# Two small rows of a fused attention kernel by DMA through device memory instead of by matmul

## What is computed

```python
# layer 0                                        # layer 1 (x is layer 0's output)
q, k = Wq@x + bq, Wk@x + bk       # 32 rows      theta = theta_w@x + theta_b;  phi = maxpool2(phi_w@x + phi_b)
v    = Wv@x + bv                  # 256 rows     g = maxpool2(g_w@x + g_b)     # 128 rows, 1024 columns
attn = softmax(q.T @ k, axis=1)   # over i       attention = softmax(theta.T @ phi, axis=-1)
x    = gamma * (v @ attn) + x                    x = gamma * (out_w@(g @ attention.T) + out_b) + x
```

## Time and profile before

| | us |
|---|---|
| median of 3 runs (2786.36 to 2790.55) | 2790.31 |
| the profiled execution | 2785.08 |
| its span, first to last instruction | 2783.3 |
| first layer of one image | 534 to 546 |
| second layer of one image (images 0 to 2; the last) | 143 to 144; 118 |

### The profile page before, as it was taken

The page is one execution under the profiler, slowest core; times in us unless marked ns, Lnnn a source line. Parts: engine busy times, 40 slices in busy tenths (PEclk is TensorE's granted clock), DMA queues, the critical chain, the costliest instruction groups (busy, mean ns, idle before and its releaser), DMA issues.

```text
span 2783.3 us, 39336 instructions
## 1 busy us (share of the span) xinstructions
PE 2693.6 (97%) x12260; PEld 2159.1 (78%) x12260; DVE 2004.2 (72%) x3303; ACT 1745.2 (63%) x3171; POOL 1956.3 (70%) x1544
## 2 busy tenths in 40 slices
PE   7999999999999999998999999999899999999988
PEld 5788888877688888887778888888767888888866
DVE  7677777767767777776776777777676777777665
ACT  5566666666756666666765566666676666666657
POOL 3677777767767767776786767777577677777768
PEclk9999999999999999999999999999999999999989
DMA  2000000012110000001211000000121000000011
GB/s 86 1 16 24 16 24 16 16 39 69 61 38 16 24 16 16 16 16 38 69 65 35 24 16 16 16 16 16 46 76 61 16 16 16 16 16 16 16 46 61
DMA packets 43194, 85.03 MB, mean 31 GB/s; under 512 B 2672, under 2 KB 2800, under 8 KB 42992
## 3 DMA queue, kind: packets, MB, share of 16 engines
q1 hardware_dynamic: 35360, 68.17, 7.2%
q10 hardware_dynamic: 7632, 14.36, 1.8%
HBM read 48.96 MB, written 33.55 MB: 30 GB/s over the span
## 4 chain that ended last, share of the span: by engine, by line
PE 87%; DVE 4%; issue 3%; ACT 3%; POOL 2%; DMA 0%; POOLq 0%; ACTq 0%; DVEq 0%
PE o_ps L821 18%; PE o_ps L824 18%; PE o_ps L825 18%; PE s_ps L798 10%; PE aux L861 9%; PE aux L835 2%; PE aux L874 2%; PE aux L870 2%; DVE mx L675 2%; PE aux L895 1%; POOL prob_l L446 1%; PE aux L839 1%; PE aux L878 1%; ACT queries L530 1%; PE o_ps L861 1%
## 5 line engine op out<-in xcount | busy, mean ns | idle before, releaser
L446 POOL TENSOR_TENSOR prob_l<-prob,prob_h 128x512 fp32r<-128x512 f32 x1280 | 1640.6, 1289 | 717.4 <-ACT prob_h L508 706.0
L505 ACT ACTIVATE prob<-s_ps 128x512 f32<-128x512 f32 x1280 | 767.3, 599 | 819.8 <-PE s_ps L798 817.2
L675 DVE TENSOR_REDUCE mx<-aux 128x1 f32<-128x512 f32 x1103 | 760.7, 690 | 424.0 <-PE aux L861 419.0
L821 PE MATMUL o_ps<-prob_h,vh 128*128 128x512 f32 x2304 | 926.8, 402 | 0.5 <-ACT prob_h L508 0.4
L824 PE MATMUL o_ps<-prob_l,vh 128*128 128x512 f32 x2304 | 904.6, 393 | 1.4 <-POOL prob_l L446 1.3
L825 PE MATMUL o_ps<-prob_h,vl 128*128 128x512 f32 x2304 | 903.1, 392 | 0.0
L637 DVE TENSOR_TENSOR acc<-prob,acc 128x512 f32<-128x512 f32 x1216 | 836.4, 688 | 26.8 <-ACT prob L505 11.4
L508 ACT ACTIVATE prob_h<-s_ps 128x512 fp32r<-128x512 f32 x1280 | 762.1, 595 | 0.0
L798 PE MATMUL s_ps<-queries,keys 128*128 128x512 f32 x1280 | 524.3, 411 | 17.9 <-DVE queries L694 10.8
L824 PEld LDWEIGHTS o_ps<-prob_l,vh 128*128 128x128 f32 x2304 | 436.7, 190 | 97.7 <-POOL prob_l L446 5.0
L825 PEld LDWEIGHTS o_ps<-prob_h,vl 128*128 128x128 f32 x2304 | 434.6, 189 | 99.7
(11 more groups left out here) (122 smaller groups left out, 1947.9 us busy)
## 6 DMA issues: line engine op xcount, KB each, us to landing
xa<-x SPq DMA_DIRECT2D x32, 512.0 KB, 3.7
spill<-xa SPq DMA_DIRECT2D x32, 512.0 KB, 2.7
xa<-spill SPq DMA_DIRECT2D x32, 512.0 KB, 3.7
y<-xa SPq DMA_DIRECT2D x32, 512.0 KB, 2.7
xp<-x ACTq DMA_DIRECT2D x26, 512.0 KB, 3.7
xp<-x SPq DMA_DIRECT2D x2, 512.0 KB, 9.1
prob<-w_in ACTq DMA_DIRECT2D x1, 576.0 KB, 5.3
wo<-w_out ACTq DMA_DIRECT2D x1, 128.0 KB, 6.1
```

Source lines behind the costliest of these rows:

```text
L446: nc.gpsimd.tensor_tensor(out=prob_l[:, i, :], in0=prob[:, i, :], in1=prob_h[:, i, :].bitcast(f32), op=ALU.subtract).then_inc(pl_ready, 1)
L505: nc.scalar.activation(prob[:, i, :], s_ps[s][:, :], ACT.Exp).then_inc(p_ready, 1)
L675: ins = nc.vector.tensor_reduce(out=dst, in_=bank[:, :], axis=AX.X, op=ALU.max)
L821: mm(o_ps[ct][:, :], value(vh, l, t, ct), prob_h[:, i, :], start=t == 0, stop=False)
```

## The change

M gets no bank for 59 of its 64 chunks, and D2 none for 59 of 64 either. For those, SP moves the values: it writes the maxima's two parts (`nm_pair`, 8 values per partition) to device memory as two rows of 512 (1024 pieces of 4 bytes), waits for the landing, and reads the two rows into rows 96 and 97 of `queries`. The reciprocals (512 pieces) go out likewise and come back as one row broadcast to 128 partitions (`rb`, 256 KB). The scores wait for the semaphore `nm_in`, VectorE's multiplication for `r_in`. SP now walks the common list, with its stores and loads at the places of `N`, `ZA` and `XL`.

In the first layer D2 moves from tile 0 to tile 4, with all that follows it up to `T1L`; M is at tile 25; the maxima end at tile 23, with two of them in tiles 0, 6 to 9 and 20 to 22. In the second layer D2 is at tile 4, Z at tiles 4 and 6, M for the next chunk at tile 0 (for chunk 1 at tile 5 of chunk 0, where its maxima have just been found). The scores matmuls take 98 rows instead of 128.

```diff
-                put(g, 1, on(Job("D2", *prev, 0), X1))
+                put(g + 4, 1, Job("D2", *prev, 0))
...
-                steps = [(i, X0) for i in range(27)] + [(i, X1) for i in range(20, 25)]
+                steps = sorted(([(0, 1, X0), (0, 1, X1)] + [(t, 3, X0) for t in range(1, 23)]
+                         + [(t, 1, X1) for t in (6, 7, 8, 9, 20, 21, 22, 23)]), key=lambda e: e[:2])
...
-                put(g + 28, 1, on(Job("M", 0, b, n + 1, 0), X1))
+                put(g + 25, 1, Job("M", 0, b, n + 1, 0))
...
-                put(g, 1, on(Job("D2", *prev, 0), X0))
+                put(g + 4, 1, Job("D2", *prev, 0))
...
-                    put(g + 2 + 2 * k, 3, on(Job("Z", *prev, k), X0))
-                    put(g + 3 + 2 * k, 3, Job("ZA", *prev, k))
+                    put(g + 4 + 2 * k, 3, on(Job("Z", *prev, k), X0))
+                    put(g + 5 + 2 * k, 2 * k + 1, Job("ZA", *prev, k))
...
-                    put(g + 1, 1, on(Job("M", 1, b, n + 1, 0), Y))
+                    put(g, 1, Job("M", 1, b, n + 1, 0))
...
-                put(g + 4, 3, on(Job("M", 1, b, 1, 0), X0))
+                put(g + 5, 1, Job("M", 1, b, 1, 0))
...
+                elif name == "M" and job in ROW_OF:
+                    i = ROW_OF[job]
+                    wait_free(sp, LAST_MAX[l, b, c])
+                    sp.dma_start(nm_rows[row].rearrange("h (s p) -> p (h s)", p=P),
+                                 nm_pair[:, :, :].bitcast(f32).rearrange("p h s -> p (h s)")).then_inc(nm_out, 16)
+                    sp.wait_ge(nm_out, 16 * (i + 1))
+                    wait(sp, nm_in, 16 * i)
+                    sp.dma_start(queries[NM, q_slot(l, b, c), :].bitcast(f32), nm_rows[row]).then_inc(nm_in, 16)
+                elif name == "D1" and Job("D2", l, b, c, 0) in ROW_OF:
+                    i = ROW_OF[Job("D2", l, b, c, 0)]
+                    wait_free(sp, job)
+                    sp.dma_start(r_rows[row].rearrange("(s p) -> p s", p=P), rsum[:, :]).then_inc(r_out, 16)
+                    sp.wait_ge(r_out, 16 * (i + 1))
+                    wait(sp, scaled, i)
+                    sp.dma_start(rb[:, :], r_rows[row:row + 1, :].broadcast_to([P, CH])).then_inc(r_in, 16)
...
+                    rows = Job("M", l, b, n, 0)
+                    if rows in BANK:
+                        wait_free(pe, rows)
+                    else:
+                        pe.wait_ge(nm_in, 16 * (ROW_OF[rows] + 1))
```

More of the change, by code:

```diff
@@ L164, in make_plan @@
+                for i, (t, place, at) in enumerate(steps):
+                    put(g + t, place, maxima(0, b, n + 1, i // SUBS, i % SUBS, at))
+                put(g + 25, 1, Job("M", 0, b, n + 1, 0))
+            else:
+                for i, (t, place, at) in enumerate([(0, 1, X0), (0, 1, X1)] + [(t, 3, X0) for t in range(1, 27)]):
+                    put(g + t, place, maxima(1, b, i // SUBS, 0, i % SUBS, at))
                 if more:
@@ L272 @@
         LAST_READ.append(Job("G1", 1, _job.b, _job.c, 0) if _job.l else Job("V0", 0, _job.b, _job.c, 1))
+    if _job.name in ("M", "D2") and _job not in BANK:
+        ROW_OF[_job] = sum(j.name == _job.name for j in ROW_OF)
     if _job.name in ("K0", "V0", "K1Q", "K1K", "T1"):
@@ L429, in _, with entry @@
                     load_a(nxt // NCH % 2, nxt // (2 * NCH), nxt % NCH)
+            def entry(job):
+                name, l, b, c, k = job
+                row = chunk_no(l, b, c)
+                if name in ("N", "ZA") and k == CT - 1:
+                    store_a(l, b, c)
+                elif name == "XL" and l == 1 and k == CT - 1:
+                    reload(0, b, c)
+                elif name == "M" and job in ROW_OF:
[13 more added lines that the diff above has]
+                    sp.dma_start(rb[:, :], r_rows[row:row + 1, :].broadcast_to([P, CH])).then_inc(r_in, 16)
+            for p in range(ASLOTS + PSLOTS):
+                load_p(p)
+            late = {}
+            with nc.allow_non_contiguous_dma(reason="rows of one value per partition"):
+                for g in range(TILES):
+                    for job in late.get(g, ()):
+                        reload(*job[1:4])
+                    for job in BEFORE.get(g, ()):
+                        entry(job)
+                    for e in DURING.get(g, ()):
+                        entry(e.job)
+                        if e.job.name == "ZA" and e.job.k == CT - 1:
+                            late.setdefault(g + 2, []).append(e.job)
+                for job in END:
+                    entry(job)
             for slot in range(ASLOTS):
@@ L682, in maximum @@
                                               op=ALU.max, negate=True))
-                chain(nc.vector.tensor_copy(nm_wide[:, :, R3], nm))
-                nc.vector.tensor_tensor(out=nm_wide[:, :, R3 + 1], in0=nm, in1=nm_wide[:, :, R3].bitcast(f32),
-                                        op=ALU.subtract).then_inc(free[BANK[job]], 1)
+                rows = Job("M", l, b, n, 0)
+                if rows in BANK:
+                    hi, lo = nm_wide[:, :, R3], nm_wide[:, :, R3 + 1]
+                else:
+                    hi, lo = nm_pair[:, 0, :], nm_pair[:, 1, :]
+                    wait(dve, nm_out, 16 * ROW_OF[rows])
+                chain(nc.vector.tensor_copy(hi, nm))
+                nc.vector.tensor_tensor(out=lo, in0=nm, in1=hi.bitcast(f32), op=ALU.subtract).then_inc(free[BANK[job]], 1)
             def entry(job):
@@ L865, in entry @@
                     for s in range(SUBS):
[L866 removed]
+                        last = mm(dst[0:R3 + 2, s * P:(s + 1) * P], nm_wide[:, s, :], ident_r[:, :], start=True, stop=True)
                 elif name == "D1":
```

108 lines of the change are left out of this document (59 added, 49 removed).

## The result

The changed kernel takes **3743.03 us** (median of 4 runs, 3739.95 to 3762.86) against 2788.8 for the kernel before on the same chip: 1.344 times as long (95% interval 1.339 to 1.349), 954 us more. The forecast was 2771, its range ended at 2840.

A forecast was written before the change was run, and what follows sets the result against it. Limits differ by stage: TensorE binds the first layer and images 0 to 2, GpSimd the last image's second layer. Terms -43.1 - 4.6 + 8.4 - 13.5 + 4.5 + 13.9 + 10.4 + 5 = -19 us; 2790.3 - 19 = 2771, range 2725 to 2840.

The forecast's parts named there:

- What a hop costs: Both layers' DMA hops: writes 2.7 us (reciprocals) and 3.0 (maxima), bounds 0.38 and 6.5; broadcast 2.9, maxima's read 2.0.
- `cols` row: Profile row of a load at the kernel's start, 128 pieces of 36 bytes, 6.5 us: taken as a write hop's upper bound.
- store row: Profile row of 512 KB stores, landing 2.7 us after issue: taken as the price of the reciprocals' write.
- the 1.0 I took: Second layer: 1.0 us added to the maxima's write for the 512 KB store ahead in its queue, bounds 0 and 2.7.
- The SP chain of the second layer: SP's serial hops take 9.8 us from reciprocal to scores; with 5.4 of work, no second-layer chunk is under 15.2 us.
- rival B: Second layer: SP's chain binds, with writes of 4.5 and 5.0 us and a floor of 19.0; about 2838 us, chance 0.28.
- First layer hidden: First-layer hops fit their allowances: maxima 5.2 us against 7.5, reciprocals 5.8 against 9.2, so nothing waits.
- both signs that I had named: Signs of a wrong forecast: the two writes land in under 2 or over 4 us, or VectorE waits for the first-layer broadcast.
- The order at no cost: First layer: D2 moved ahead of the doubled maxima on VectorE costs 0.3 us a chunk, bounds 0 and 0.9; +8.4 us.
- 1.54 us of TensorE a chunk: TensorE work removed per chunk: M 0.63 us and D2 0.91; over 28 first-layer chunks -43.1 us.
- 98 partitions for 128: Scores matmuls contracting over 98 partitions and not 128 cost and save nothing: 96 take 401 ns, 128 take 411.
- The clock: Second layer: waits bring 3.3 us at half clock, losing 1.65 each; charged once in chunk 0 to 1, plus +5 us.

The follow-up runs named there:

- runs16: The changed kernel with column 4p+s of a chunk belonging to partition p, so both writes go in 16-byte runs: 3052.8 us, 1.096 times the kernel before.
- const_rows: The changed kernel without its four hops, constants in place of the two rows, new order kept: 2935.6 us, 1.053 times the kernel before.
- const_three: const_rows with the second bank's last maxima one tile later, second-layer D2 at tile 2, first-layer multiplication reading PSUM: 2809.2 us, ratio 1.008 to before.
- m16: Kernel before, with only the maxima sent by DMA in 16-byte runs and first-layer maxima ending two tiles earlier; reciprocals by matmul: 2875.1 us, ratio 1.032.
- both_writes: The changed kernel, but in the second layer SP issues the next maxima's write right behind the reciprocals' write: 3565.1 us in one run.

## Why the prediction was wrong

- **What a hop costs: the step that failed.** I had no row of 4-byte pieces and bounded a write by the `cols` row, 36-byte pieces, from above, then took values near the store row. Measured: 9.26 us for the reciprocals in the chunk shown and 10.8 for the maxima in the median, outside the bounds of both. A row of pieces of another size, and of a load, was no bound for these writes: at 16 bytes the hop is 1.6 us, at 4 packed bytes 9.5. What stands ahead in the queue costs more than the 1.0 I took, too: in `runs16` the write of the maxima took 5.87 us behind the broadcast and the store, 1.6 to 2.8 without them, and the broadcast had no part in my 1.0.
- **The rule that I weighed against the change** (the Trainium skill, DMA: Bandwidth & Descriptors, Specifications: below 512 B a read-modify-write, off line rate) pointed the right way, but size is not what prices it here: 16-byte runs took 1.6 us, spaced 4-byte pieces 1.9, packed ones 9.5.
- **The SP chain of the second layer: right as a mechanism, mis-sized.** Order, members and the floor that takes the place of all other bounds came as written; rival B is what happened. By its own rule, 28 us per microsecond on both writes, 7.1 us more on each (9.1 and 10.8 in the median) give 2771 + 199 = 2970. The rest of the loss lies where B saw none: it counted 12 to 16 chunks, and all 28 behind the second layers' first ones became 32 to 39 us; the first layer was taken as hidden.
- **First layer hidden: failed through the same price.** The allowances were right (7.2 measured for M against 7.5; 9.9 for D2 against 9.2). M's two hops of 12.9 us did not fit, and D2's of 14 did not either: VectorE waited for the broadcast 4.5 us at most, 28 times. With that, both signs that I had named for a wrong forecast came.
- **The order at no cost: failed on its own account.** I charged the moved D2 0.3 us a chunk. The runs show three costs in the list of places: `rb` puts VectorE's operand in SBUF (26 us), D2 four tiles later pushes `T1L` into the tile where the next maxima need its bank (53 us), and Z stands in D2's own tile (50 us). The places could be read from the diff: each moved job's successor on its bank, and where its operand now lies. Their prices are known from these runs only.
- **1.54 us of TensorE a chunk: too high, by the price of D2.** The earlier trace rows compared the first step of a chunk with the second; in `const_rows` that step, without D2 but with one maximum more (0.24), still takes 2.46 us against 2.74, so D2 was worth 0.5 and not 0.91. M was priced right: its two steps take 2.10 and 1.73 us before and 1.61 each in `const_rows`, together 0.6. Of these 1.1 us `const_three` gained 0.4 a chunk, 64.3 to 63.9. The step that holds the multiplication (2.05 against 1.84) and the one with the last maximum (2.02 against 1.84) take 0.4 back, and many others are some 0.02 us longer each; why is open.
- **98 partitions for 128: right.** The mean of a scores matmul is 411 ns before and 413 in `m16`.
- **The clock: right in kind, far too small.** I counted four stretches of 3.3 us at half clock. The granted clock of the second-layer chunks above is 0.69 to 0.70, that of the first-layer chunk 0.94, and the stretches at half clock add up to some 970 us in the whole span, against 89 before (mean granted clock 0.870 and 0.984).

## What to carry over

Before a transpose goes through device memory, count the bytes that lie together at the destination: here packed 4-byte pieces cost some 8 us more than 16-byte runs, and a layout that makes runs moves the stride to TensorE's loads. Price a reordered schedule apart from what it makes room for, by running it with constants: here it cost some 150 us before any hop was paid. A matmul that hides in a full pipeline is worth the step it really lengthens, found by comparing the same step with and without it.

## What the runs showed of the hardware

- Writes of packed 4-byte pieces took 7.6 to 11.3 us for 128 to 2048 of them; 8 bytes apart 3.0 to 3.9, 32 apart 1.9 to 2.1. Gathering 1024 pieces 64 bytes apart back into two rows took 5.8 to 7.1.
- A short write behind a 256 KB broadcast and a 512 KB store in the same queue landed after 5.87 us instead of 1.6 to 2.8, and stores of 512 KB among slow writes took 9.8 in the median instead of 2.7.
- Two packed 4-byte writes issued some 1.2 us apart (`both_writes`) landed side by side in 15 of 27 cases (9 to 11 us for the second) and one after the other in 12 (16 to 19).
- float32 weight loads with columns 16 bytes apart: 325 ns against 191.
- `scalar_tensor_tensor` on 128 x 512 float32 beside a busy GpSimd: 1264 ns with both tensors in SBUF, 745 with one in PSUM; with GpSimd mostly idle 749 with both in SBUF.
